# A wait for the edge list ahead of the loads of the weights and of x, in a gated graph network on one core

## The reference

```python
h = jnp.maximum(_layernorm(x, axis=-1), 0.0)
for _ in range(5):
    messages = h[col] @ W_msg.T + b_msg          # col = dst
    agg = segment_sum(messages, row)             # row = src
    gi = agg @ W_ih.T + b_ih
    gh = h @ W_hh.T + b_hh
    r, z = sigmoid(i_r + h_r), sigmoid(i_z + h_z)
    n = tanh(i_n + r * h_n)
    h = (1 - z) * n + z * h
out = x + h
```

## Time and profile before

| | |
|---|---|
| time, median of 3 runs (lowest to highest) | 5238.51 us (5238.23 to 5245.75) |
| time of the profiled execution | 5244.7 us |
| its span | 5242.9 us |
| TensorE busy | 4932.7 us (94%) |
| GpSimd busy | 3763.1 us (72%) |
| VectorE busy | 2568.6 us (49%) |
| ScalarE busy | 861.6 us (16%) |
| granted TensorE clock, mean | 0.98 |

### The profile page before, as it was taken

The page is one execution under the profiler, slowest core; times in us unless marked ns, Lnnn a source line. Parts: engine busy times, 40 slices in busy tenths (PEclk is TensorE's granted clock), DMA queues, the critical chain, the costliest instruction groups (busy, mean ns, idle before and its releaser), DMA issues. The chain is left out here.

```text
span 5242.9 us, 80270 instructions
## 1 busy us (share of the span) xinstructions
PE 4932.7 (94%) x26501; PEld 2515.3 (48%) x26502; DVE 2568.6 (49%) x7000; ACT 861.6 (16%) x1421; POOL 3763.1 (72%) x3869
## 2 busy tenths in 40 slices
PE   5588888699998999999999999999999999999998
PEld 1344444344444455555545555555555555555554
DVE  8899993366666533333334333333333333333332
ACT  7666662000000000000000000000000000000000
POOL 3777777777777777677767777777767777767774
PEclk7799999899999999999999999999999999999999
DMA  5255555466666766666676766676676667565654
GB/s 172 67 165 164 165 164 167 115 174 176 175 173 168 208 178 180 191 178 175 181 202 178 191 178 176 181 199 189 175 194 175 179 183 210 179 193 181 188 179 125
DMA packets 1036728, 916.10 MB, mean 175 GB/s; under 512 B 507905, under 2 KB 771453, under 8 KB 1036412
## 3 DMA queue, kind: packets, MB, share of 16 engines
q1 hardware_dynamic: 482262, 661.95, 40.8%
q0 software_dynamic: 123920, 212.72, 15.2%
q10 hardware_dynamic: 430358, 39.09, 6.1%
HBM read 766.27 MB, written 147.15 MB: 174 GB/s over the span
## 5 line engine op out<-in xcount | busy, mean ns | idle before, releaser
L725 POOL DMA_INDIRECT f_ring<-fast_hrows,f_work x3160 | 3068.7, 971 | 1140.4 <-issue 940.7
L1018 PE MATMUL f_ps_a<-f_ring,f_hr 128*128 128x512 fp8e4 (+1 forms) x13560 | 3024.1, 375 | 11.1 <-DMA f_ring<-fast_adj 6.8
L1018 PEld LDWEIGHTS f_ps_a<-f_ring,f_hr 128*128 128x128 f16 x13560 | 1305.3, 98 | 1472.1 <-issue 146.9
L1533 DVE TENSOR_SCALAR f_ring<-f_iota_h,f_work 128x128 f16<-128x128 f16 (+1 forms) x3120 | 588.3, 284 | 986.3 <-PE f_ps_a L1030 957.9
L703 POOL DMA_INDIRECT fast_rec<-f_slots x656 | 644.8, 983 | 214.3 <-issue 199.6
L1458 DVE SCALAR_TENSOR_TENSOR f_work<-f_deg,f_bias_c,f_ps_c 128x512 f32<-128x512 f32 x125 | 93.4, 748 | 1017.7 <-PE f_ps_deg L1057 1017.7
L1030 PE MATMUL f_ps_a<-f_ring 128*128 128x128 f16 (+1 forms) x5616 | 507.2, 232 | 57.5 <-DMA f_ring<-fast_hrows,f_work 57.4
L1030 PEld LDWEIGHTS f_ps_a<-f_ring 128*128 128x128 f16 x5616 | 421.7, 98 | 251.8 <-DMA f_ring<-fast_hrows,f_work 65.5
L821 ACT ACTIVATE f_work<-f_work,f_bsum 128x512 f32<-128x512 f32 x125 | 90.2, 722 | 2202.1 <-DVE f_work L1458 2202.1
L1408 DVE TENSOR_SCALAR f_ring<-f_iota_h,f_work 128x256 f16<-128x256 f16 x1536 | 412.1, 358 | 0.0
L977 PE MATMUL f_ps_deg<-f_ring,f_sel 128*128 128x512 fp8e4 x1536 | 394.8, 380 | 0.0
(11 more groups left out here) (334 smaller groups left out, 3185.6 us busy)
## 6 DMA issues: line engine op xcount, KB each, us to landing
f_ring<-fast_adj SPq DMA_DIRECT2D x750, 640.0 KB
fast_adj<-f_ring SPq DMA_DIRECT2D x192, 512.0 KB
f_ring<-fast_hrows,f_work POOLq DMA_INDIRECT x3160
f_deg<-fast_deg SPq DMA_DIRECT2D x125, 256.0 KB
fast_hrows<-f_work ACTq DMA_DIRECT2D x400, 64.0 KB
f_hr<-fast_hrows SPq DMA_DIRECT2D x24, 640.0 KB, 7.5
fast_rec<-f_slots POOLq DMA_INDIRECT x656
fast_hrows<-f_deg SPq DMA_DIRECT2D x1, 6528.0 KB, 35.3
```

The source lines that it names most:

```text
L725: nc.gpsimd.indirect_dma_start(tile_rows(cls, g), None, hrows, bass.IndirectOffsetOnAxis(ap=idx_tab[:, col + g:col + g + 1], axis=0)).then ...
L1018: mm = pe.matmul(sumT[buf][:, 0:cols], lhsT=hr[:, t, a * H:(a + 1) * H], rhs=a_f8[:, t * CHUNK:t * CHUNK + cols], start=(t == 0 and a == 0 ...
L1533: ins = nc.vector.tensor_scalar(tile_hots(cls, g, w), iota_h[:, 0:w], loc[:, bass.ds(col + g, 1)], HOT, ALU.is_equal, ALU.mult)
```

## The change

SyncE now waits for the first memset only, loads dst, then waits until the three list gathers have landed, and for the other two memsets, and only then issues the weights, the biases, x and the fill. The zeros of the row table get a second wait, until all 24 group gathers have landed.

```diff
         @block.sync
         def _(sp):
-            sp.wait_ge(pads_ready, 3)
+            sp.wait_ge(pads_ready, 1)
             sp.dma_start(dfull[0:ROWS, 0:K], dst.rearrange("(p k) -> p k", k=K)).then_inc(dst_loaded, 16)
             sp.dma_start(dfull[0:ROWS - 1, K:K + 2], dst.rearrange("(p k) -> p k", k=K)[1:ROWS, 0:2]).then_inc(dst_loaded, 16)
+            sp.wait_ge(list_loaded, 48)
+            sp.wait_ge(pads_ready, 3)
             sp.dma_start(wmsg_sb, W_msg).then_inc(weights_loaded, 16)
...
             sp.dma_start(rec_dram.rearrange("(p t) o -> p (t o)", p=P)[:, 0:T2C], fill).then_inc(rec_filled, 16)
             sp.wait_ge(consts_ready, 1)
+            sp.wait_ge(groups_loaded, 16 * 2 * GK)
             for first, last in ((0, N1), (NT * P, 2 * NPAD)):
```

## The result

The changed kernel takes 5246.6 us (median of 21 runs) against 5238.5 us before (22 runs of that kernel). A 22nd run of it, at a mean granted clock of 0.556 where the others had 0.98, took 8730.9 us and is left out. The ratio of the two kernels is 1.0015, with a 95% interval from 1.0009 to 1.0021, so the changed one is 4.7 to 11 us slower, 7.9 us in the middle. The profiled execution has 5246.2 us, its span 5244.3 us. The forecast was 6.7 us more, within 0.2% of before.

The account below looks back on a forecast made before the run. The prediction took the set-up to bound the kernel: the first scatter's start moves the end one to one. From 5238.5 us, 6.0 us gained and 12.6 us of new wait gave +6.7, so 5245.2 us; range 5240 to 5253 us.

Parts of the forecast that it names:

- dst sooner and alone: SyncE's dst load: 1.0 us from earlier issue, 1.2 us from travelling alone (bounds 0.4 and 1.6), together 2.2 us gained.
- The list without x: The list gathers before VectorE's one-hot columns: 3.8 us gained without x beside them, bounds 0 and 5.2 us.
- Weights: 4.7 us: Ten weight and bias loads in SyncE's queue between list and x: 4.7 us taken, high end 10.05 us.
- x: 12.3 us: x from issue to landing: 12.3 us, between 10.9 (low end, 2.2 us for gathers beside it) and 13.1 (profile row).
- rival 1: SyncE's queue between list and x: the weights keep their stalls, counts 12.8 us late, 5251.3 us; chance 0.14.
- The counts: ScalarE's counts of dwin, behind its sums of x: VectorE waits 12.6 us at column 32, goes on at about 74.0 us.
- Rival 4: At column 32: x comes so soon that VectorE never waits for the counts; 6.0 us gained, 5232.5 us; chance 0.08.
- The zeros: The row table's zeros, stored later beside the first 19 scatters: no cost taken; upper end 1.50 us a scatter.
- Rivals 2 and 3: 2: list no quicker, dst's early issue alone gained, 5251 us, chance 0.04; 3: zeros slow 19 scatters, 5255 us, chance 0.04.
- TensorE's wait for the first gather 7 us longer: A sign that the forecast is right: TensorE's 43.5 us wait for the first gathered rows grows by 7 us.

Follow-up runs that it names:

- e5: The changed kernel with the wait for the list moved behind the ten weight and bias loads, so x alone waits for it; 5242.5 us, ratio 1.0004.
- e3: The kernel before, without the change, with ScalarE's wait for dwin and 12 counts moved ahead of its row sums of x; 5238.5 us, ratio 0.9996.
- e6: The kernel of e2 with one more wait on SyncE's queue: x is issued only when dwin has landed; 5231.0 us, ratio 0.9985 to the kernel before.
- e2: The changed kernel with ScalarE's wait for dwin and 12 counts moved ahead of its row sums of x; 5235.0 us, ratio 0.9990 to the kernel before.
- e4: The changed kernel without the wait for the group gathers ahead of the zeros, so these leave early; 5247.7 us, ratio 1.0009 to the kernel before.
- e1: The changed kernel with the first piece of x issued ahead of the weights and biases, both behind the list wait; 5253.3 us, ratio 1.0025.

## Why the prediction was right

**dst sooner and alone: 2.2 us, measured 2.18** (14.06 to 11.88 us). The issue gave the 1.0 us that was worked out (3.71 to 2.68 us). For being alone 1.2 us was taken; against e5 it is 0.7 us, and profiles of the kernels that load dst alone use it between 11.58 and 11.88 us, so 0.7 to 1.0 us. The term was a little large, within its bounds. That the sum hit 2.18 us is partly luck of one profile: in e3, which loads dst as the kernel before does, dst is used 0.48 us sooner than in the earlier trace rows. The upper bound was also worked out wrongly: 6.6 us and half of 3.3 us are 8.25 us and not 8.7, a gain of 2.1 us and not 1.6.

**The list without x: 3.8 us, measured 4.5** (6.66 us on the use of the list, less 2.18). The gather landed in 2.6 us, not in the 3.3 us taken from the main phase. The Trainium skill ("DMA: Bandwidth & Descriptors", Queues, rings and completion order) says that a DMA engine serves the queues in turn, a whole packet of one before the next. The 7.1 us beside x and the 2.6 us without it agree with that; it is not shown that packets are the reason.

**Weights: 4.7 us, measured 5.2; x: 12.3 us, measured 12.3.** W_hh stood 0.48 us in the queue instead of 4.29, and 3.56 us again in e5, where dst is ahead of it; so it was dst that had held it, and rival 1 falls. The list came 0.6 us sooner than forecast (23.03 us for 23.6) and the weights took 0.5 us longer; that x was issued at 28.16 us for the forecast 28.3 is luck by that much. For x's landing the row was the better guide: in e6, with no large gather beside it, x takes 12.2 us, so the company cost about 0.9 us of the 13.1 and not the 2.2 of the low end. The Trainium skill's formula ("DMA: Bandwidth & Descriptors", Anatomy of one DMA), given for GpSimd's queue and worked out as an estimate of 11.0 us for x, is 1.2 us short of e6; the measurement decides.

**The counts: VectorE goes on at 74.0 us, measured 73.68, after 12.9 us of waiting for the 12.6 forecast.** First scatter: forecast about 124 us, measured 123.46. This was the step on which all hung, and e2 shows that it is the cause and not only beside it: taking x out of the way of the counts turns the sign of the change. Rival 4 falls with the 12.92 us.

**The zeros: nothing, and nothing measured** (e4); the scatters beside them take 0.97 us. Rivals 2 and 3 fall with the list's 2.6 us and with e4.

**Wrong in what would show it:** "TensorE's wait for the first gather 7 us longer". The waits of the changed kernel are these:

```profile
DVE f_work L1436 <- DMA f_late<-fast_rec: 124.5, 1, 124.5
...
PE f_ps_a L1033 <- DMA f_ring<-fast_hrows,f_work: 48.8, 5, 45.1
```

They grew by 1.1 and 1.6 us against the earlier trace rows, not by 7. The building of the dense blocks had moved too, on a path of its own. ScalarE does the statistics of the rows behind its counts (67.01 us before, 73.68 us now), the low halves of the rows follow them, and the building waits until SyncE has stored these (issued at 207.04 us before, 213.76 us now). So TensorE and VectorE came to their waits some 6 us later. I had the statistics 6.9 us late in my sum and left the building where it was.

That these are two paths is seen in e2, where they part. The first instruction of the building, on VectorE, in the kernel before, in the changed kernel and in e2:

```profile
218.12 0.43 DVE L1396 COPY f_ps_m<-f_iota_h 128x256 f32<-128x256 f32 x1 [11.09 <-DMA fast_hrows<-f_ring]
...
224.62 0.43 DVE L1399 COPY f_ps_m<-f_iota_h 128x256 f32<-128x256 f32 x1 [10.87 <-DMA fast_hrows<-f_ring]
...
230.88 0.43 DVE L1397 COPY f_ps_m<-f_iota_h 128x256 f32<-128x256 f32 x1 [11.18 <-DMA fast_hrows<-f_ring]
```

The waits in e2:

```profile
DVE f_work L1434 <- DMA f_late<-fast_rec: 105.3, 1, 105.3
...
PE f_ps_a L1031 <- DMA f_ring<-fast_hrows,f_work: 29.2, 4, 25.4
```

In e2 the building begins 12.8 us later than before while the scatters begin 5.5 us sooner, and TensorE's wait for the first gather shrinks from 43.5 to 25.4 us. The late x is paid there out of this slack, and 25.4 us of it are left.

**Wrong in rival 4:** x ahead of the weights was named as a way out. e1 shows that it is the opposite, because ScalarE's program order has the weights in front of x. I had read that order for x and the counts, and not for the weights. The rival's figure was wrong as well: x at 34.0 us lets VectorE go on at 67.3 us, as before; to gain the 6.0 us x would have to be there at 61.4 - 33.3 = 28.1 us.

The profiled executions differ by only 1.4 us in span though the first gather comes 7.7 us later. The first gathers' difference agrees with the ratio (7.9 us). What made the profiled main phase of the kernel before 6 us longer stays open; that execution was itself 6.2 us over its median.

## What to carry to other kernels

When a transfer is put off to speed up another one, list who waits for it in the program order of each engine, and add up the whole of that engine's work behind it: here 33 us of sums and counts hung on x, and had no slack, while the building of the dense blocks hung on it too and had 43 us of it. Two paths that meet within half a microsecond gain nothing when only one is shortened; change the order on the other one first, or with it (e2, e6), and expect that order alone to bring nothing (e3). A marker well upstream, such as the start of the first scatter, orders variants that differ by less than the runs of one kernel do.

## What was not expected of the hardware

- A large load on one queue holds gathers on another. A gather of one word per row, 0.5 KB in all, landed in 7.1 us beside x and in 2.6 us without it; dwin (608 KB) landed in 9.8 us beside x in e2 and in 5.0 us without it in e6. For the gather of 0.5 KB its bytes cannot be the reason.
- DMAs stand in SyncE's queue behind a large one: 6.08 us for a bias of half a KB behind x in e1, 4.29 us for W_hh behind dst, 0.48 us for W_hh with neither. It is not the next one that stands: in e1 the three weights directly behind x stood 0.42 to 0.58 us each. What fills up stays open.
- dst alone is hardly faster than with the weights beside it (0.7 to 1.0 us, above). The window of the changed kernel shows five of sixteen engines' share again, at 136 GB/s where the earlier trace rows had 129:

```profile
8.50:10.50 2.00, 0.00 (x0) 0.00 (x0) 0.23 (x15) 0.00 (x0) 0.00 (x0) 1.00 0.32 136
```

The Trainium skill ("DMA: Bandwidth & Descriptors", Why a DMA increments its semaphore by 16 and not by 1) says that a DMA is split over the largest number up to 16 that divides the outer dimension of both its sides. For dst's 125 rows that is 5, and the share of 0.32 agrees. A load of dst in rows that 16 divides was not tried.
